# Cross-attention and ternary FFN on one core: squared queries in bf16 halves, a new order of every engine's two turns, weight chunks in two buffers

## The chip, the core and the metric

The kernel runs on one core of a Trainium2 chip. The metric is the device time of one execution in microseconds (us), lower is better. A core has TensorE (PE; its weight loads are listed as PEld), VectorE (DVE), ScalarE (ACT), GpSimd (POOL) and SyncE (SP), which issues every DMA here. Each engine works through its own list in order, and they meet at semaphores.

## The reference

```python
x = x + tanh(g_xattn[0]) * xattn(layernorm(x), ctx_1024, Wq, Wk, Wv, Wo, gq, gk)
x = x + tanh(g_ffn[0]) * ffn(layernorm(x), w_gate, w_up, w_down)

# xattn: 32 batch rows, 100 queries, 361 keys, 16 heads of 128
q = rmsnorm(hidden @ Wq, gq); k = rmsnorm(ctx @ Wk, gk); v = ctx @ Wv
out = softmax(q k^T / sqrt(D)) v @ Wo
# ffn: weights ternary: round(w / mean|w|) clipped to -1..1, times mean|w|
#      activations rounded to 8 bits per row; silu(gate) * up, then down
```

x is 32x100x512, ctx_1024 is 32x361x256, Wq is 512x2048, Wk and Wv are 256x2048, Wo is 2048x512, the three FFN matrices have 2048x512 elements each.

## The kernel before, in words

`attention_block` handles two batch rows (a pair) at a time, 16 pairs `i` in all; `ffn_block` follows. A factor of a product is held as a bf16 high half and a bf16 low half, and `product` makes three matmuls of them. A pair has 8 units: head group (4 heads) `u // 2` of batch row `u % 2`. While the values of unit `u` are mixed, unit `u+1` is scored and the keys of unit `u+2` are made, so that in turn `u` all three stages run. Two turns, odd `u` and `v = u + 1`, stand in one hand-written list per engine, `two_turns(i, u)`; a pair has four such double turns, `u` = 1, 3, 5, 7.

Keys of a unit are three tiles `t` (128, 128, 105 rows). PE: `keys`; ACT: `keys_square`; DVE: `sum_keys`; POOL: `key_scale` (two instructions); DVE: `scale_keys`; ACT: `keys_hi`; POOL: `keys_lo`; SP: `turn_keys`, a DMA transpose into `kT`; then PE may run `scores`. Query projections of a head group are made once in a double turn (`queries(i, u, 0)` and `1`), and `query_squares` sums the squares over the 128 partitions by a matmul: the f32 squares `qsq` are its weights, a column of ones is what moves. `query_squares_out` (DVE) and `query_scale` (POOL) make `qrs` of it, which `row_bias` of a later unit needs.

Queries, mixed values (`m`), head outputs (`o`), turned x (`x`) and squared-query sums (`qss`) take turns in two PSUM banks, `shared_ps`, in the order that `shared_uses` lists. `shared_bank` makes PE wait until the use two before has been read out (`shared_free`). In the double turn `u` = 3 the next pair's x is turned (`turn_x`), read out by `turn_x_hi` on ACT and `turn_x_lo` on DVE.

SP's list is `turn(i, u)`, one call for every unit: load a chunk, turn the context (in turns 5 and 6, `turn_ctx(i+1, b, ..)`, which `keys` of units 8 and 9 wait for through `ctxT_in`), turn keys, turn probabilities (`turn_probs`), and last `store_chunk`.

The FFN weights are made ternary beside attention, in 48 chunks of 128x512, one in a turn. In pairs 1 to 6 each chunk is loaded and its absolute values are summed (`weight_chunk` on ACT). In pairs 8 to 13 each is loaded again, scaled on ACT, clipped and rounded on POOL (`round_chunk`, w_rounded), and stored by SP (`store_chunk`), which first waits:

```python
sp.wait_ge(w_rounded, m + 1)
```

The lines that the rows name: L23 to L25 are the three matmuls of `product`; L527 the matmul of `query_squares`; L667 a copy to a high half on ACT; L716 `queries_square`; L877 a low half on DVE; L893 `scale_keys`; L917 `row_sum`; L923 `probs_lo`; L949 `layernorm`; L966 `query_squares_out`; L1181 `keys_lo`; L1221 and L1226 the clip and the rounding of `round_chunk`; L292 `turn_ctx`; L309 `turn_keys`; L372 `load_chunk`; L379 `store_chunk`.

## Time and profile before

| what | value |
| --- | --- |
| three runs | 2347.47 us median, 2344.13 to 2347.76 |
| the profiled execution | 2351.92 us, its span 2350.1 us, mean granted TensorE clock 0.977 |
| start and pair 0 | 0 to 210.9 us of the span |
| pairs 1 and 2 (chunks summed) | 210.92 to 455.61 us, 122.3 us a pair |
| pairs 3 to 7 (chunks summed until pair 6) | 455.61 to 1075.73 us, 124.0 us a pair |
| pairs 8 to 13 (chunks rounded) | 1075.73 to 1827.44 us, 125.3 us a pair |
| pairs 14 and 15 | 1827.44 to 1951.18 and 1951.18 to 2057.74 us |
| `ffn_block` | the last 292.4 us |

The borders of the pairs are the starts of the copies of the projected output (`project_out`), one couple of them at the end of each pair. The first row compares executions; everything else is of the one profiled execution. Matmuls overlap in the records, so that the cost of one is read from start to start, not from its duration. A few keys matmuls are missing in the records (136 to 137 of 144 stand in a pair); the time that they took is there as a hole without a releaser.

### The profile page before, as it was taken

The page shows a single profiled execution, that of the slowest core. Times are in us where ns is not written, and L with a number is a line of the kernel's source. Part 1 is how long each engine was busy: PE and PEld are TensorE (multiplying, and loading weights), DVE is VectorE, ACT ScalarE, POOL GpSimd, SP SyncE. Part 2 cuts the span into 40 slices and gives each one's busy share as a digit, 9 for nine tenths or more (in the row PEclk, how much of TensorE's full clock was granted, in tenths as well). Part 3 has the DMA queues.
Part 4 walks back from the last instruction along what each step waited for, and adds up shares of the span by engine and source line. Part 5 has one row for each costly group of instructions (what it writes and reads, how often), then busy time and mean ns, then how long its engine had stood idle before and what let it go on. Part 6 is the DMA issues. An engine that isn't in the chain of part 4 may idle for free. (4 is left out here: it accounts for less than half of the span.)

```text
span 2350.1 us, 45689 instructions
## 1 busy us (share of the span) xinstructions
PE 2215.9 (94%) x16187; PEld 1573.9 (67%) x16338; DVE 1837.9 (78%) x4171; ACT 1612.3 (69%) x3398; POOL 1273.9 (54%) x1623
## 2 busy tenths in 40 slices
PE   5889999999999999999999999999999999769999
PEld 3567777777776777777777777776767777534444
DVE  5788877787777787877777778777777777569997
ACT  4677777777776777666767777676767667546665
POOL 4555656565656555656666676767666655200000
PEclk9899999999999999999999999999999999989999
DMA  5776776666677776656676767676777665635665
GB/s 144 169 149 136 124 146 127 139 133 129 131 130 144 123 144 126 132 105 139 132 145 136 151 129 149 135 138 134 143 145 132 133 109 111 171 95 139 141 140 126
DMA packets 921748, 317.53 MB, mean 135 GB/s; under 512 B 864912, under 2 KB 882608, under 8 KB 921264
## 3 DMA queue, kind: packets, MB, share of 16 engines
q1 hardware_dynamic: 921520, 314.61, 66.6%
q8 instruction: 129, 2.11, 0.4%
q14 instruction: 99, 0.81, 0.1%
HBM read 82.09 MB, written 19.40 MB: 43 GB/s over the span
## 5 line engine op out<-in xcount | busy, mean ns | idle before, releaser
L1181 POOL TENSOR_TENSOR ksplit<-khat,ksplit 128x512 bf16<-128x512 f32 (+1 forms) x384 | 455.5, 1188 | 74.0 <-ACT ksplit L667 73.1
L893 DVE TENSOR_TENSOR khat<-keys_ps,krs 128x512 f32<-128x512 f32 (+1 forms) x384 | 263.4, 686 | 287.4 <-POOL krs L1175 287.2
L1175 POOL TENSOR_TENSOR krs<-kvar,minus_half 128x4 f32<-128x4 f32 (+1 forms) x384 | 387.1, 1008 | 32.0
L689 ACT ACTIVATE prob<-score_ps,nbias,qrs 100x361 f32<-100x361 f32 x512 | 328.6, 647 | 71.8 <-DVE nbias L911 70.4
L1172 POOL TENSOR_SCALAR kvar<-kss 128x4 f32<-128x4 f32 (+1 forms) x384 | 89.1, 232 | 531.9 <-DVE kss L883 530.0
L672 ACT ACTIVATE ksq<-keys_ps 128x512 f32<-128x512 f32 (+1 forms) x384 | 227.8, 596 | 188.5 <-PE keys_ps L25 188.4
L698 ACT ACTIVATE psplit<-prob,rden 100x361 bf16<-100x361 f32 x512 | 304.3, 595 | 64.9 <-DVE rden L917 64.2
L923 DVE SCALAR_TENSOR_TENSOR psplit<-prob,rden,psplit 100x361 bf16<-100x361 f32 x512 | 317.5, 629 | 4.2 <-ACT psplit L698 0.6
L901 DVE TENSOR_REDUCE nmax<-score_ps 100x1 f32<-100x361 f32 x512 | 268.3, 524 | 54.5 <-PE score_ps L25 54.3
L667 ACT ACTIVATE ksplit<-khat 128x512 bf16<-128x512 f32 (+1 forms) x384 | 240.5, 626 | 98.0 <-DVE khat L893 97.3
L24 PE MATMUL keys_ps<-wk_split,ctxT 128*128 128x512 bf16 (+1 forms) x768 | 293.8, 383 | 6.8
L25 PE MATMUL keys_ps<-wk_split,ctxT 128*128 128x512 bf16 x767 | 293.2, 382 | 0.0
L23 PE MATMUL keys_ps<-wk_split,ctxT 128*128 128x512 bf16 (+1 forms) x642 | 247.8, 386 | 33.3 <-DVE khat L893 18.3
L883 DVE TENSOR_REDUCE kss<-ksq 128x4 f32<-128x512 f32 (+1 forms) x384 | 259.6, 676 | 15.4 <-ACT ksq L672 15.2
L23 PE MATMUL shared_ps<-pT,nat 128*128 128x400 bf16 (+1 forms) x768 | 257.4, 335 | 10.7 <-DVE qT_lo L956 5.4
L23 PE MATMUL shared_ps<-xT_hi,wq_split 128*128 128x200 bf16 x1024 | 257.5, 251 | 9.6 <-DVE wq_split L877 5.7
L24 PE MATMUL shared_ps<-xT_lo,wq_split 128*128 128x200 bf16 x1024 | 257.6, 252 | 0.0
L25 PE MATMUL shared_ps<-xT_hi,wq_split 128*128 128x200 bf16 x1024 | 257.5, 251 | 0.0
L25 PE MATMUL shared_ps<-pT,nat 128*128 128x400 bf16 (+1 forms) x768 | 256.4, 334 | 0.0
L24 PE MATMUL shared_ps<-pT,nat 128*128 128x400 bf16 (+1 forms) x768 | 256.2, 334 | 0.0
L23 PE MATMUL y_ps<-oT_hi,wo_hi 128*128 128x200 bf16 x1024 | 255.0, 249 | 0.5 <-DVE oT_lo L877 0.5
L24 PE MATMUL y_ps<-oT_lo,wo_hi 128*128 128x200 bf16 x1024 | 255.0, 249 | 0.0
(132 smaller groups left out, 5323.1 us busy)
## 6 DMA issues: line engine op xcount, KB each, us to landing
stage<-in_ffn SPq DMA_DIRECT2D x96, 256.0 KB, 3.2
ctx_raw<-in_ctx SPq DMA_DIRECT2D x31, 256.0 KB, 3.5
xin<-in_x SPq DMA_DIRECT2D x32, 200.0 KB
res_rows<-in_x SPq DMA_DIRECT2D x32, 200.0 KB
x_rows<-res_rows SPq DMA_DIRECT2D x32, 200.0 KB
xin<-x_rows SPq DMA_DIRECT2D x25, 256.0 KB, 2.7
xres<-x_rows SPq DMA_DIRECT2D x25, 256.0 KB, 3.0
out<-xres SPq DMA_DIRECT2D x25, 256.0 KB, 2.0
```

The source lines that it names most:

```text
L23: pe.matmul(out, w_hi, m_hi, start=first, stop=False)
L24: pe.matmul(out, w_hi, m_lo, start=False, stop=False)
L25: return pe.matmul(out, w_lo, m_hi, start=False, stop=last)
L667: return act.activation(out, in_, ACT.Copy)
L689: act.activation(prob[:, h, :], score_ps[h % 2][0:SQ, 0:SK], ACT.Exp, bias=nbias[:, b, h:h + 1], scale=qrs[:, v // 2 % 2, r:r + 1], accum_ ...
L698: act.activation(psplit[0:SQ, h // TWO, 0, h % TWO, 0:SK], prob[:, h, :], ACT.Copy, scale=rden[:, b, h:h + 1]).then_inc(p_hi_done, 1)
L883: dve.tensor_reduce(kss[0:KV[t], k, :], ksq[0:KV[t], k, :].rearrange("p (h d) -> p h d", h=G), AX_X, ALU.add).then_inc(kss_done, 1)
L893: dve.tensor_tensor(khat[0:KV[t], k, :].rearrange("p (h d) -> p h d", h=G), keys_ps[k][0:KV[t], :].rearrange("p (h d) -> p h d", h=G), rs, ...
L901: dve.tensor_reduce(nmax[:, b, h:h + 1], score_ps[h % 2][0:SQ, 0:SK], AX_X, ALU.max, negate=True).then_inc(nmax_done, 1)
L923: dve.scalar_tensor_tensor(out=psplit[0:SQ, h // TWO, 1, h % TWO, 0:SK], in0=prob[:, h, :], scalar=rden[:, b, h:h + 1], in1=psplit[0:SQ, h ...
L1175: pool.tensor_tensor(krs[0:KV[t], k, :], kvar[0:KV[t], k, :], minus_half[0:KV[t], 0:G], ALU.pow).then_inc(krs_done, 1)
L1181: pool.tensor_tensor(ksplit[0:KV[t], t, 1, :], khat[0:KV[t], (u + t) % 2, :], ksplit[0:KV[t], t, 0, :], ALU.subtract).then_inc(k_lo_done, 1)
```

## The change

The squares of the queries are written twice by ACT: f32 into `qsq` (now only two heads, reused) and bf16 into `qsq_hi`; POOL subtracts them into the bf16 `qsq_lo`. `query_squares` multiplies high and low halves of 128 columns each. `qss` moves behind the head outputs. The lists of PE, ACT, DVE and POOL are put in a new order. Weight chunks use two buffers (stage slots 0 and 3) and are loaded a turn ahead; weight staging has 6 slots in place of 7. The context of batch row 0 is loaded for the pair after the next one at the end of turn 6, that of row 1 in turn 2.

```diff
             if more_queries(u, last):
-                order += [("q", u, 0)]
-            if more_queries(u, last):
-                order += [("q", u, 1)]
+                order += [("q", u, 0), ("q", u, 1)]
             order += [("m", u, 0), ("m", u, 1)]
             if u == UNITS - 5 and not last:
                 order += [("x", 0)]
-            if more_queries(u, last):
-                order += [("qss", u)]
             order += [("o", v, 0), ("o", v, 1)]
             if u == UNITS - 5 and not last:
                 order += [("x", 1)]
+            if more_queries(u, last):
+                order += [("qss", u)]
...
-    OWN_STAGES = 5
+    OWN_STAGES = 4
...
# SP: load_chunk, turn
             def load_chunk(i, u):
+                i, u = (i, u + 1) if u < UNITS else (i + 1, 1)
                 n, m = sum_chunk_of(i, u), tern_chunk_of(i, u)
-                if n is not None and n > 0:
-                    sp.wait_ge(w_summed, n)
-                if m is not None:
-                    sp.wait_ge(w_summed, MATRICES * CHUNKS)
-                    if m > 0:
-                        sp.wait_ge(w_rounded, m)
                 if n is not None or m is not None:
+                    c = n if m is None else MATRICES * CHUNKS + m
+                    if m is not None:
+                        sp.wait_ge(w_summed, min(c - 1, MATRICES * CHUNKS))
+                        if m > 1:
+                            sp.wait_ge(w_rounded, m - 1)
+                    elif n > 1:
+                        sp.wait_ge(w_summed, n - 1)
                     rows, cols = chunk_at(n if m is None else m)
-                    sp.dma_start(w_raw[:, :], w_ffn[rows, cols]).then_inc(w_raw_in, 16)
+                    sp.dma_start(w_raw[c % 2], w_ffn[rows, cols]).then_inc(w_raw_in[c % 2], 16)
...
                 if not last and u == 1:
-                    sp.wait_ge(nat_ready, (i * 2 + 2) * KVT)
-                    load_ctx(i + 1, 0, ctx_raw)
...
+                if not last and u == 2:
+                    sp.wait_ge(nat_ready, (i * 2 + 3) * KVT)
+                    load_ctx(i + 1, 1, ctx_raw)
+                if i < PAIRS - 2 and u == UNITS - 2:
+                    sp.wait_ge(nat_ready, (i * 2 + 4) * KVT)
+                    load_ctx(i + 2, 0, ctx_raw)
                 store_chunk(i, u)
...
# PE: query_squares
-                eng.wait_ge(q_sq_done, i * (NG * QD) + ((u + 3) // 2 + 1) * QD)
+                eng.wait_ge(q_sqlo_done, i * (NG * QD) + ((u + 3) // 2 + 1) * QD)
                 for b in range(2):
                     for h in range(G):
-                        last = pe.matmul(ps[0:SQ, b * G + h:b * G + h + 1], qsq[:, h, b * SQ:(b + 1) * SQ],
-                                         ones[:, 0:1], start=True, stop=True)
+                        out, hi, lo = ps[:, b * G + h:b * G + h + 1], h * QT + b * SQ, (G + h) * QT + b * SQ
+                        pe.matmul(out, qsq_split[:, hi:hi + P], ones[:, 0:1], start=True, stop=False)
+                        last = pe.matmul(out, qsq_split[:, lo:lo + P], ones[:, 0:1], start=False, stop=True)
...
# ACT and POOL: the new passes
+            def queries_square_hi(i, u, k):
+                n, p = use(i, ("q", u, k))
+                ps, heads = shared_ps[p][:, 0:TWO * QT].rearrange("p (h q) -> p h q", h=TWO), slice(k * TWO, (k + 1) * TWO)
+                eng.wait_ge(shared_done, n + 1)
+                act.activation(qsq_hi[:, heads, :], ps, ACT.Square).then_inc(q_sqhi_done, 1)
...
+                eng.wait_ge(q_sq_done, n)
+                eng.wait_ge(q_sqhi_done, n)
+                pool.tensor_tensor(qsq_lo[:, heads, :], qsq[:, :, :], qsq_hi[:, heads, :],
+                                   ALU.subtract).then_inc(q_sqlo_done, 1)
```

The order of a double turn after the change, the lists written without their conditions (`u` and `v = u + 1`; keys are those of `u+2` and `v+2`, scores, maxima and probabilities those of `u+1` and `v+1`):

```
PE    keys u:0, u:1; queries 0; scores 0; queries 1; keys u:2; scores 1, 2; keys v:0; mixed u 0, 1;
      scores 3; keys v:1; [turn_x 0]; heads_out 0, 1; [turn_x 1]; keys v:2; query_squares;
      scores v 0, 1; project 0 to 3; scores v 2, 3; mixed v 0, 1
DVE   sum u:0, u:1; row_max 0, row_bias 0; scale u:0, u:1; queries_lo 0; sum u:2; row_max 1, row_sum 0,
      row_bias 1; queries_lo 1; scale u:2; row_max 2; [layernorm 0]; row_sum 1; sum v:0; row_bias 2;
      mixed_lo 0; row_max 3; mixed_lo 1; row_bias 3, probs_lo 0, row_sum 2; scale v:0; [layernorm 1];
      probs_lo 1, row_sum 3; [turn_x_lo 0]; heads_out_lo 0; probs_lo 2, 3; heads_out_lo 1; [turn_x_lo 1]; ...
POOL  key_scale u:0, u:1, keys_lo u:0; query_squares_lo 0; key_scale u:2, keys_lo u:1, u:2;
      key_scale v:0; [split_ctx 0]; query_squares_lo 1; [split_ctx 1, 2]; keys_lo v:0,
      key_scale v:1, v:2; keys_lo v:1, v:2; round_chunk u; query_scale; round_chunk v
```

In brackets stands what one double turn of a pair alone has. Before, PE ran `query_squares` ahead of `heads_out`, `keys v:0` between the two `mixed`, and `scores 0, 1` together; POOL had `round_chunk u` behind `key_scale v:0` and `query_scale`, ahead of all three `keys_lo v`.

## Rows read from the trace of the kernel before

**Rows 1.** The page's first part: busy time, share of the span, instructions.
```profile
PE 2215.9 (94%) x16187; PEld 1573.9 (67%) x16338; DVE 1837.9 (78%) x4171; ACT 1612.3 (69%) x3398; POOL 1273.9 (54%) x1623
```

**Rows 2.** Windows, three groups of pairs: length, busy PE, PEld, DVE, ACT, POOL; clock; DMA.
```profile
210.92:455.61 244.69, 238.50 (x1875) 178.48 (x1889) 194.95 (x449) 178.07 (x405) 148.40 (x186) 1.00 0.70 135
455.61:1075.73 620.12, 606.86 (x4693) 455.58 (x4732) 488.52 (x1124) 442.20 (x996) 370.92 (x461) 0.98 0.68 130
1075.73:1827.44 751.71, 725.69 (x5630) 543.85 (x5677) 584.81 (x1345) 532.95 (x1164) 508.31 (x646) 0.99 0.71 140
```

**Rows 3.** Waits of PE in pairs 8 to 13: us in total, times, longest.
```profile
PE shared_ps L23 <- DVE qvar L966: 7.6, 6, 2.3
PE keys_ps L23 <- DVE khat L893: 7.3, 11, 1.1
...
PE shared_ps L23 <- DVE xT_lo L877: 4.1, 6, 0.7
```

**Rows 4.** Groups of weight loads by shape: busy us, mean ns, idle before.
```profile
L25 PEld LDWEIGHTS y_ps<-oT_hi,wo_lo 128*128 128x128 bf16 x1024 | 100.2, 98 | 0.0
...
L24 PEld LDWEIGHTS score_ps<-kT,qT_hi 128*100 128x100 bf16 x512 | 64.3, 126 | 12.5 <-issue 0.2
```

**Rows 5.** Timeline of PE: start, length; first and last of 24 output projections.
```profile
1011.43 0.25 PE L23 MATMUL y_ps<-oT_hi,wo_hi 128*128 128x200 bf16 x1
...
1013.41 0.25 PE L25 MATMUL y_ps<-oT_hi,wo_lo 128*128 128x200 bf16 x1
```

**Rows 6.** Timeline of PE: a burst of squared-query matmuls and what follows it.
```profile
1593.86 1.49 PE L527 MATMUL shared_ps<-ones,qsq 128*100 128x1 f32 x16
1595.21 0.25 PE L23 MATMUL shared_ps<-uT,wv_hi 128*128 128x200 bf16 x1
```

**Rows 7.** Windows: behind the burst of pair 7's turn 3, and in pair 15.
```profile
1003.00:1009.80 6.80, 6.27 (x35) 5.29 (x35) 4.21 (x10) 2.63 (x5) 5.28 (x6) 0.50 0.47 90
...
2044.05:2050.88 6.83, 5.52 (x17) 2.49 (x18) 0.57 (x1) 0.50 (x1) 0.00 (x0) 0.50 0.98 317
```

**Rows 8.** Timeline of PE: the longest idle stretch of pair 15 ends.
```profile
2045.36 0.49 PE L23 MATMUL shared_ps<-pT,nat 128*128 128x400 bf16 x1 [5.29 <-DMA pT<-psplit]
```

**Rows 9.** Timeline of POOL: a chunk's rounding at the end of turn 6, pair 12.
```profile
1671.22 1.16 POOL L1181 TENSOR_TENSOR ksplit<-khat,ksplit 105x512 bf16<-105x512 f32 x1 [0.34 <-ACT ksplit L667]
...
1673.53 0.70 POOL L1226 TENSOR_SCALAR w_out<-stage 128x512 bf16<-128x512 f32 x1 [0.16 <-POOL stage L1221]
```

**Rows 10.** Timeline of PE: second keys matmul of turn 7, and its first scores.
```profile
1674.58 0.38 PE L24 MATMUL keys_ps<-wk_split,ctxT 128*128 128x512 bf16 x1
...
1679.01 0.32 PE L23 MATMUL score_ps<-kT,qT_hi 128*100 128x361 bf16 x1
```

**Rows 11.** Timeline of SP's queue: the end of turn 5 and the start of turn 6.
```profile
1666.03 0.41 SPq L379 DMA_DIRECT2D w_tern<-w_out  x1
...
1667.03 3.81 SPq L292 DMA_TRANSPOSE ctxT<-nat  x3
1670.93 3.98 SPq L309 DMA_TRANSPOSE kT<-ksplit  x3
```

**Rows 12.** DMA issues: count, median us from issue to landing.
```profile
ctxT<-nat SPq DMA_TRANSPOSE x96, 3.0
```

**Rows 13.** Groups by line, ACT, POOL and DVE: busy us, mean ns, idle before.
```profile
L716 ACT ACTIVATE qsq<-shared_ps 128x400 f32<-128x400 f32 x128 | 64.4, 503 | 108.6 <-PE shared_ps L25 108.6
...
L1181 POOL TENSOR_TENSOR ksplit<-khat,ksplit 128x512 bf16<-128x512 f32 (+1 forms) x384 | 455.5, 1188 | 74.0 <-ACT ksplit L667 73.1
...
L923 DVE SCALAR_TENSOR_TENSOR psplit<-prob,rden,psplit 100x361 bf16<-100x361 f32 x512 | 317.5, 629 | 4.2 <-ACT psplit L698 0.6
...
L893 DVE TENSOR_TENSOR khat<-keys_ps,krs 128x512 f32<-128x512 f32 (+1 forms) x384 | 263.4, 686 | 287.4 <-POOL krs L1175 287.2
...
L949 DVE TENSOR_SCALAR xin<-xin,ln_mv,ln_rstd 100x512 f32<-100x512 f32 x32 | 18.8, 590 | 0.0
...
L877 DVE TENSOR_TENSOR xT_lo<-shared_ps,xT_hi 128x400 bf16<-128x400 f32 x32 | 18.2, 569 | 1.6 <-ACT xT_hi L667 1.2
```

More of the change, by code:

```diff
@@ L116, in use, with query_use @@
         return i * USES + k, k % 2
+    def query_use(i, u):
+        n = i * UNITS + u // 2 * 2 - 3
+        return use(n // UNITS, ("q", n % UNITS, QD - 1))[0]
     def unit(i, u):
@@ L406, in turn @@
                         load_x(i + 1, b, xin, x_in)
-                if not last and u == 3:
-                    sp.wait_ge(nat_ready, (i * 2 + 3) * KVT)
-                    load_ctx(i + 1, 1, ctx_raw)
                 if not last and u in (UNITS - 3, UNITS - 2):
@@ L601, in two_turns @@
                 if su:
-                    scores(i, u + 1, 0), scores(i, u + 1, 1)
+                    scores(i, u + 1, 0)
+                if qu:
+                    queries(i, u, 1)
                 if ku:
                     keys(i, u + 2, 2)
-                if qu:
-                    queries(i, u, 1)
                 if su:
-                    scores(i, u + 1, 2)
-                mixed(i, u, 0, par)
+                    scores(i, u + 1, 1), scores(i, u + 1, 2)
+                if kv:
+                    keys(i, v + 2, 0)
+                mixed(i, u, 0, par), mixed(i, u, 1, par)
                 if su:
                     scores(i, u + 1, 3)
-                if kv:
-                    keys(i, v + 2, 0)
-                mixed(i, u, 1, par)
                 if kv:
@@ L1046, in two_turns @@
                     layernorm(i, 0)
-                if qu:
-                    queries_lo(i, u, 1)
                 if su:
-                    row_max(i, u + 1, 3), row_bias(i, u + 1, 2), row_sum(i, u + 1, 1), probs_lo(i, u + 1, 0)
-                    row_bias(i, u + 1, 3)
-                mixed_lo(i, u, 0)
+                    row_sum(i, u + 1, 1)
                 if kv:
@@ L1055, in two_turns @@
                 if su:
-                    probs_lo(i, u + 1, 1), row_sum(i, u + 1, 2)
+                    row_bias(i, u + 1, 2)
+                mixed_lo(i, u, 0)
+                if su:
+                    row_max(i, u + 1, 3)
                 mixed_lo(i, u, 1)
+                if su:
+                    row_bias(i, u + 1, 3), probs_lo(i, u + 1, 0), row_sum(i, u + 1, 2)
                 if kv:
                     scale_keys(i, v + 2, 0)
+                if new_x:
+                    layernorm(i, 1)
                 weights_lo(pieces_of(i, u, 1))
+                if su:
+                    probs_lo(i, u + 1, 1), row_sum(i, u + 1, 3)
                 if new_x:
-                    layernorm(i, 1), turn_x_lo(i, 0)
-                if qu:
-                    query_squares_out(i, u)
+                    turn_x_lo(i, 0)
+                weights_lo(pieces_of(i, u, 2)), heads_out_lo(i, v, 0)
                 if su:
-                    row_sum(i, u + 1, 3), probs_lo(i, u + 1, 2)
-                if kv:
-                    sum_keys(i, v + 2, 1)
-                if su:
-                    probs_lo(i, u + 1, 3)
-                weights_lo(pieces_of(i, u, 2))
-                heads_out_lo(i, v, 0), heads_out_lo(i, v, 1)
+                    probs_lo(i, u + 1, 2), probs_lo(i, u + 1, 3)
+                heads_out_lo(i, v, 1)
+                if new_x:
+                    turn_x_lo(i, 1)
                 if i == TERN_PAIR - 1 and u == 1:
                     weight_scales()
-                if new_x:
-                    turn_x_lo(i, 1)
                 if u == 1 and not last:
@@ L1079, in two_turns @@
                 if sv:
-                    row_max(i, v + 1, 0), row_bias(i, v + 1, 0), row_max(i, v + 1, 1), row_bias(i, v + 1, 1)
+                    row_max(i, v + 1, 0)
+                if kv:
+                    sum_keys(i, v + 2, 1)
+                if sv:
+                    row_bias(i, v + 1, 0)
                 if kv:
@@ L1093, in two_turns @@
                 if sv:
-                    probs_lo(i, v + 1, 0), probs_lo(i, v + 1, 1), row_sum(i, v + 1, 2), row_sum(i, v + 1, 3)
+                    probs_lo(i, v + 1, 0), row_sum(i, v + 1, 2), row_sum(i, v + 1, 3), probs_lo(i, v + 1, 1)
                 weights_lo(pieces_of(i, v, 1))
@@ L1204, in split_ctx @@
                     eng.wait_ge(ctx_in[b], (j + 1) * 32)
-                    if not (isinstance(j, int) and j == 0):
-                        eng.wait_ge(shared_done, use(j - 1, ("m", 1, CC - 1))[0] + 1)
+                    if j > 1:
+                        eng.wait_ge(shared_done, use(j - 2, ("m", UNITS - 1, CC - 1))[0] + 1)
                 pool.tensor_copy(nat[0:KV[t], par, b, t, 0, :], raw[0:KV[t], t, :]).then_inc(nat_hi_done, 1)
```

201 lines of the change are left out of this document (114 added, 87 removed).

## The prediction

> **What bounds the kernel now.** I read the page first: PE is busy for 94% of the span, no other engine over 78% [rows 1]. Durations of matmuls overlap, so I went on to the windows by pair: PE stands idle for some 3% of a pair (6.2 of 244.7 us in pairs 1 and 2, 26.0 of 751.7 in pairs 8 to 13), while DVE is busy for 78 to 80% and ACT for 71 to 73% [rows 2]. Attention is bound by PE's list, and a change is worth what it takes out of PE's starts and PE's idle time. A pair takes 122.3, 124.0 and 125.3 us in the three groups. The middle group differs from the first by the granted clock (0.98 against 1.00), the last by waits. The waits of PE in the last group are 23.4 us in six pairs, 3.9 a pair, with the wait of the squared-query matmul on `mixed_lo` (0.7 us in each pair); the largest kinds are in [rows 3]. The same view gives 2.3 a pair for the others, of the same kinds.
>
> **The cheaper squares.** A burst of 16 f32 matmuls with one moving column takes 1.35 us from its start to the next group's start [rows 6], 84 ns each; there are 64 bursts, so 86 us. The new burst has 16 bf16 matmuls too, each behind a load of 128 columns. No row shows such loads back to back. From above: among 200-column matmuls a load of 128 hides wholly, and these follow each other by 1.98 / 23 = 86 ns [rows 5]; from below only nothing bounds it. A burst costs 0.91 us. Gain 64 x 0.44 = 28 us; ends -2 (a loss) and 86.
>
> The Trainium skill (TensorE: Matmul & The Clock Gate, Weight-path perf modes) says that the fast weight load is on when the number of weights is 128 and the type is not FP32, measured at about twice the speed. The trace agrees with the direction (98 against 126 ns). By the page's other figure, a plain load of one column in 1/1.2 ns, half of 107 ns for 128 columns is an estimate of 53 ns, and a gain of 32 us.
>
> **The added passes.** ACT gets one more Square of 503 ns for each query use [rows 13], 8 a pair, 4.0 us on some 88 of 125 busy. POOL gets 8 subtractions of 400 columns, 1188 x 400/512 = 0.93 us each [rows 13], 7.4 us a pair on 508.3 / 6 = 84.7 [rows 2]. Neither bounds a pair. DVE gets nothing. What is exposed is order, so I walked a double turn with the durations of the rows. From keys u:0 at 0 us, without stalls, PE runs scores 0 at 4.7, mixed 0 at 10.7, scores 3 at 13.7, the head outputs at 15.5 and 16.5, keys v:2 at 17.6, the squares at 18.9 and ends at 28.6. `mixed_lo` 1 ends at 15.5 on DVE, khat u:0, u:1, u:2 and v:0 at 6.8, 7.5, 12.2 and 17.1: each just ahead of its reader. An ordinary double turn has no stall over some 0.2 us; uncovered, each of these would cost its lateness once a double turn.
>
> **The turn with the new x (u = 3).** Here a wait is added. `heads_out` 1 stands two uses behind `turn_x` 0 in the shared banks, so it waits for `turn_x_lo` 0. On DVE this stands behind `mixed_lo` 1 with row_bias 3, probs_lo 0, row_sum 2, scale v:0, layernorm 1, probs_lo 1 and row_sum 3 between: 0.2 + 0.63 + 0.15 + 0.69 + 0.59 + 0.63 + 0.15 = 3.0 us, then 0.57 of its own [rows 13]. `mixed_lo` 1 ends at 16.0 in this double turn (a layernorm lies ahead of it), so the bank is free at 19.6, and PE wants it at 17.0: 2.6 us, where before the same place cost 0.73 + 0.69 (4.1 us in six pairs behind xT_lo [rows 3]). Small stalls of the other double turns I put at 0.5. So 3.1 a pair against 2.3: +0.8 in eight pairs without rounding (1 to 7 and 14) is +6 us. Bounds: 0.5 and 5 a pair.
>
> **The clock.** Behind the burst of `u` = 3 the granted clock is 0.50, its lower level of 1.2 GHz, for 6.8 us, in which the 24 head-output matmuls run [rows 7]: 24 x 86 ns = 2.1 us lost. Ahead of it PE had four transposes, a wait, the burst with one moving column, and another wait. It happens in pairs 3 to 14, so 12 x 2 = 24 us less a few that overlap idle time: 22. The change moves the burst away from the transposes, but sets an idle 2.6 us near them. I take half of it: gain 11, ends 0 and 22.
>
> **The queue behind the rounding.** This is the step that speaks against the change. `store_chunk(i, u)` makes SP wait for `w_rounded` at the end of turn u, and everything of turn v is queued behind: in turn 6 three `turn_ctx`, in each turn v three `turn_keys`, and `turn_probs`. Before, the rounding of chunk u stood ahead of `keys_lo v`. Now POOL reaches it only behind `keys_lo` v:2. Before, that very slot held the rounding of chunk v: keys_lo ends at 1672.4, the rounding at 1674.23 [rows 9], while the next double turn starts at 1674.58 - 0.21 = 1674.37 [rows 10]. So w_rounded now comes about when the next double turn starts; I move it 0.6 us earlier, for keys v:2 ends 9.9 us before the end in place of some 9.2. From the store to the third context transpose's issue SP takes 1.0 + 2/3 x 3.81 = 3.5 us [rows 11], and landing takes 3.0 [rows 12], 6.5 in all, while keys u:0 of turn 7 (unit 9) need all three. Stall: 6.5 - 0.1 - 0.6 = 5.8; since the trace also shows shorter landings in this place I take 5.2. In the other three double turns the queue has the store, a load and three key transposes, 6.6 us, and the first scores stand 4.64 us behind the start [rows 10]: 6.6 - 0.6 - 4.6 = 1.4 at most, less in the first double turn, where `keys_lo` ends earlier; I take 0.8, so 2.4. An idle 5.29 us in pair 15 [rows 8] was followed by 0.50 for 6.83 us, 5.5 of them busy [rows 7]: 2.7 lost; I take 2.0. Sum 9.6 us a pair; with the 3.1 above 12.7, against 3.9 before: +8.8, six pairs, +53 us. Ends of the 9.6: 0 where the transposes land in time after all, and 6.3 + 3.4 + 3 x 2.0 = 15.7.
>
> The Trainium skill (TensorE: Matmul & The Clock Gate, Why this matters for your kernels) wants no idle gap of TensorE over about 3 us, lest the clock falls back to half. The trace agrees (5.29 us idle, then 0.50), and by this rule the wait of turn 7 costs more than its idle time.
>
> **The rest.** Double chunk buffers: ACT never waited for a chunk, so nothing. The context two turns ahead takes a wait of POOL away, which reached PE as a part of the 7.6 us behind qvar [rows 3]; that is inside the 3.9 that I replace. Six staging slots in place of seven and the extra passes in the start: +2 us, ends 0 and 6. `ffn_block` is untouched.
>
> Sum: -28 + 6 - 11 + 53 + 2 = +22 us on the profiled 2351.9, so 2374; the median of the runs is 0.19% lower, so 2369.5, rounded to 2369.
>
> **Rivals** (times on the scale of the median). (1) The other side: the transposes behind the rounding land in time, because POOL gets to it earlier than in my walk. Then the rounding pairs get 3.1 - 3.9 = -0.8 each and the sum is -36: 2311. For it: DVE and ACT have slack of a fifth; against: the slot of [rows 9]. It decides where the queue costs under 6.0 us a pair rather than 9.6. (2) The queue costs its upper end, 15.7: +36 us more, 2405. (3) The walk is wrong in `u` = 3: no long wait for xT_lo, and the clock stays up: -2 x 15 - 11 = -41, 2328. For it, two waits of 0.7 there became one; against, seven instructions on DVE. (4) Full-width loads are no faster: 28 us more, 2397; the 98 ns speak against it. (5) The change doesn't do what it might for the clock: 0.50 behind the turned x in every pair, 11 more, 2380. (6) The in-order lists stall by themselves, 2 us a pair: 30 more, 2399.
>
> **How the numbers follow.** Chances: forecast (2350 to 2390) 0.36, (1) 0.20, (2) 0.12, (3) 0.12, (4) 0.06, (5) 0.08, (6) 0.06. The range 2300 to 2405 reaches to (1) and (2). A measurement of this kernel tells about 0.2%, 4.7 us, from no change. Faster: (1) 0.20, of (3) 0.10, of the forecast 0.02: 0.32. Same: 0.10, of the forecast's lower edge and of (3). Slower: the rest, 0.58.
>
> **What would show it.** In the profile after: 16 squared-query matmuls in some 1.0 us; in pairs 8 to 13 a wait of `keys_ps` L23 on the DMA ctxT<-nat of about 5 us, one a pair, with clock 0.50 behind it, and waits of `score_ps` on the DMA kT<-ksplit; none of these in pairs 1 to 7; one wait of `shared_ps` on xT_lo of 2 to 3 us a pair; pairs without rounding at some 119 to 121 us, those with it at about 133. The forecast is wrong first of all if SP's queue isn't what PE waits for in pairs 8 to 13.

## The result, and the profile after

The kernel after takes 2487.53 us (median of 4 runs, 2480.23 to 2491.64) against 2345.8 of the kernel before (4 runs, 2342.74 to 2347.76): a ratio of 1.0602, 95% interval 1.0573 to 1.0631. It is slower, as forecast, but by 142 us in place of 22, and it lies far above the range of 2300 to 2405.

The first part of the page after, for [rows 1]:

```profile
PE 2210.0 (89%) x16338; PEld 1517.1 (61%) x16338; DVE 1970.1 (79%) x4171; ACT 1666.7 (67%) x3526; POOL 1366.9 (55%) x1752
```

PE is busy for about as long as before, in a span of 2485.0 us in place of 2350.1: what came in is idle time. The windows of the same groups of pairs, for [rows 2] (length, busy PE, PEld, DVE, ACT and POOL, granted clock, DMA share, GB/s):

```profile
209.80:460.71 250.91, 234.82 (x1893) 171.00 (x1892) 214.20 (x450) 184.90 (x419) 158.51 (x202) 0.99 0.73 132
460.71:1083.60 622.89, 587.72 (x4733) 428.83 (x4732) 528.28 (x1125) 458.23 (x1037) 395.18 (x501) 0.99 0.71 129
1083.60:1958.99 875.39, 748.70 (x5679) 532.61 (x5677) 642.12 (x1345) 556.71 (x1213) 546.60 (x693) 0.94 0.62 119
```

Start and pair 0 lost nothing (209.8 against 210.9 us), pairs 1 to 7 lost 9.0 us (873.8 against 864.8), the six pairs that round chunks lost 123.7 (875.4 against 751.7, or 145.9 a pair in place of 125.3), pairs 14 and 15 another 3.3. That is 134.9 with the start, the whole difference of the spans. Where the six pairs lost it stands in the waits of PE in them (us in total, times, longest), for [rows 3]:

```profile
PE keys_ps L23 <- DMA ctxT<-nat: 50.3, 12, 5.6
PE score_ps L23 <- DMA kT<-ksplit: 41.4, 19, 3.4
PE shared_ps L23 <- DVE xT_lo L899: 14.0, 6, 2.3
PE shared_ps L23 <- DVE qT_lo L980: 13.1, 18, 0.7
PE shared_ps L23 <- DVE uT L899: 7.9, 18, 0.6
```

Together 126.7 us where there were 23.4: 103.3 more. The squares gave back 24 x 0.95 = 22.8 us (below). The other 43.2 us go with the clock: at a mean of 0.94 in place of 0.99, 0.06 x 875.4 - 0.01 x 751.7 = 45.0 us more of such loss is an estimate. A run below, `e9_combined_ctx`, has the same matmuls in these pairs at a mean of 1.00, and there PE is busy for 701.9 us in place of 748.7: 46.8 less. In pairs 1 to 7 the same view reads:

```profile
PE shared_ps L23 <- DVE xT_lo L899: 16.3, 7, 2.3
PE shared_ps L23 <- DVE uT L899: 11.7, 25, 0.6
PE shared_ps L23 <- DVE qT_lo L980: 11.4, 15, 1.1
PE keys_ps L23 <- DMA ctxT<-nat: 8.7, 9, 1.7
PE score_ps L23 <- DMA kT<-ksplit: 3.1, 4, 1.2
```

51.2 us, some 7.3 a pair where before had 2.3: +35, against 28 x 0.95 = 26.6 saved by the squares. So two things have to be explained: the DMA waits of the rounding pairs, and small waits on DVE in every pair.

The queue, at the end of turn 2 of pair 11. POOL first (start, length), then SP's queue, then PE:

```profile
1550.94 2.27 POOL L1217 TENSOR_TENSOR ksplit<-khat,ksplit 128x512 bf16<-128x512 f32 x2
1553.30 0.91 POOL L1266 TENSOR_SCALAR stage<-stage 128x512 f32<-128x512 f32 x1
1554.36 0.62 POOL L1271 TENSOR_SCALAR stage<-stage 128x512 bf16<-128x512 f32 x1 [0.16 <-POOL stage L1266]
```

```profile
1555.01 0.35 SPq L395 DMA_DIRECT2D w_tern<-stage  x1
1555.47 0.37 SPq L388 DMA_DIRECT2D stage<-in_ffn  x1
1555.93 3.96 SPq L319 DMA_TRANSPOSE kT<-ksplit  x3
```

```profile
1553.85 0.38 PE L23 MATMUL keys_ps<-wk_split,ctxT 128*128 128x512 bf16 x1
...
1562.04 0.54 PE L23 MATMUL score_ps<-kT,qT_hi 128*100 128x361 bf16 x1 [3.37 <-DMA kT<-ksplit]
```

The last `keys_lo` ends at 1553.21, the rounding at 1554.98, and the three key transposes, two of whose tiles had been ready for 8 and 3 us, are issued only behind the store. PE reaches the first scores at 1558.67 and waits for 3.37 us. Then the window around it has the lower level of the clock:

```profile
1561.17:1568.00 6.83, 5.96 (x30) 4.86 (x31) 2.47 (x5) 1.86 (x4) 3.17 (x4) 0.50 1.05 215
```

The new burst of squares, for [rows 6], and what follows it:

```profile
857.71 0.17 PE L547 MATMUL shared_ps<-ones,qsq_split 128*128 128x1 bf16 x1
857.74 0.16 PE L548 MATMUL shared_ps<-ones,qsq_split 128*128 128x1 bf16 x1
...
858.09 0.16 PE L548 MATMUL shared_ps<-ones,qsq_split 128*128 128x1 bf16 x1
858.11 0.34 PE L23 MATMUL score_ps<-kT,qT_hi 128*100 128x361 bf16 x1
```

16 matmuls, each behind a load of 128 columns, in 0.40 us, 25 ns each, where the f32 burst took 1.35 (its eight f32 matmuls stand in the trace as 16 records, 84 ns each). That is 0.95 us less, 64 x 0.95 = 61 us.

### The profile page after: what moved, and what is told of

It reads as the page before. It is cut to its first block and busy times, and to the rows that moved or that the text cites. A ratio compares the mean times of both kernels' runs of the same rounds, so it can differ in the third digit from the quotient of the medians.

```text
span 2485.0 us, 46479 instructions
## 1 busy us (share of the span) xinstructions
PE 2210.0 (89%) x16338; PEld 1517.1 (61%) x16338; DVE 1970.1 (79%) x4171; ACT 1666.7 (67%) x3526; POOL 1366.9 (55%) x1752
## 5 line engine op out<-in xcount | busy, mean ns | idle before, releaser
L1217 POOL TENSOR_TENSOR ksplit<-khat,ksplit 128x512 bf16<-128x512 f32 (+1 forms) x384 | 446.3, 1164 | 387.8 <-ACT ksplit L683 383.7
L23 PE MATMUL keys_ps<-wk_split,ctxT 128*128 128x512 bf16 (+1 forms) x768 | 304.7, 397 | 81.9 <-DMA ctxT<-nat 76.8
L945 DVE SCALAR_TENSOR_TENSOR psplit<-prob,rden,psplit 100x361 bf16<-100x361 f32 x512 | 323.9, 643 | 16.1 <-ACT psplit L714 16.1
L714 ACT ACTIVATE psplit<-prob,rden 100x361 bf16<-100x361 f32 x512 | 297.5, 594 | 32.1 <-DVE rden L939 25.3
L24 PE MATMUL keys_ps<-wk_split,ctxT 128*128 128x512 bf16 (+1 forms) x768 | 303.0, 395 | 0.0
L25 PE MATMUL keys_ps<-wk_split,ctxT 128*128 128x512 bf16 (+1 forms) x768 | 301.2, 392 | 0.0
L933 DVE TENSOR_TENSOR nbias<-nmax,qrs 100x1 f32<-100x1 f32 x512 | 276.6, 540 | 13.9 <-DVE nmax L923 0.5
L23 PE MATMUL shared_ps<-xT_hi,wq_split 128*128 128x200 bf16 x1024 | 263.3, 257 | 10.0 <-DVE wq_split L899 6.2
L24 PE MATMUL shared_ps<-xT_lo,wq_split 128*128 128x200 bf16 x1024 | 263.1, 257 | 0.0
L25 PE MATMUL shared_ps<-xT_hi,wq_split 128*128 128x200 bf16 x1024 | 262.9, 257 | 0.0
L1208 POOL TENSOR_SCALAR kvar<-kss 128x4 f32<-128x4 f32 (+1 forms) x384 | 74.6, 194 | 335.6 <-DVE kss L905 335.1
```

Of the source, the lines that this page charges most:

```text
L23: pe.matmul(out, w_hi, m_hi, start=first, stop=False)
L24: pe.matmul(out, w_hi, m_lo, start=False, stop=False)
L25: return pe.matmul(out, w_lo, m_hi, start=False, stop=last)
L714: act.activation(psplit[0:SQ, h // TWO, 0, h % TWO, 0:SK], prob[:, h, :], ACT.Copy, scale=rden[:, b, h:h + 1]).then_inc(p_hi_done, 1)
L933: dve.tensor_tensor(nbias[:, b, h:h + 1], nmax[:, b, h:h + 1], qrs[:, v // 2 % 2, r:r + 1], ALU.mult).then_inc(nbias_done, 1)
L945: dve.scalar_tensor_tensor(out=psplit[0:SQ, h // TWO, 1, h % TWO, 0:SK], in0=prob[:, h, :], scalar=rden[:, b, h:h + 1], in1=psplit[0:SQ, h ...
```

## The experiments

Each ratio is of the kernel to the kernel before, with its 95% interval; the kernel before was timed again for each group of runs (medians of 2350.8 to 2352.2 us). "After" is 2487.5 us, 1.0602.

| run | edit | us | ratio |
| --- | --- | --- | --- |
| `e1_store_behind_keys` | after; store u and the load of turn v behind the transposes of turn v | 2349.2 | 0.9987 (0.9971 to 1.0004) |
| `e2_rounding_early` | after; chunk u scaled and rounded where it was before | 2361.0 | 1.0065 (1.0041 to 1.0089) |
| `e3_swap_dve` | after; queries_lo 1 ahead of row_bias 1 | 2455.2 | 1.0442 (1.0414 to 1.0471) |
| `e4_xlo_early` | after; turn_x_lo 0 ahead of layernorm 1 | 2460.9 | 1.0468 (1.0441 to 1.0496) |
| `e14_short_keys_lo` | after; one keys_lo of six cut to a quarter | 2423.9 | 1.0308 (1.0272 to 1.0344) |
| `e6_hundred_columns` | after; loads of 100 columns | 2493.2 | 1.0601 (1.0569 to 1.0633) |
| `e5_old_order` | bf16 squares in the lists of before | 2447.5 | 1.0410 (1.0386 to 1.0434) |
| `e10_old_lo_early` | e5; query_squares_lo 1 earlier on POOL | 2386.6 | 1.0148 (1.0117 to 1.0180) |
| `e11_old_squares_late` | e10; squares behind the head outputs | 2367.5 | 1.0063 (1.0043 to 1.0083) |
| `e8_combined_two_out` | e1 + e3 + e4, two buffers for rounded chunks | 2310.8 | 0.9832 (0.9811 to 0.9853) |
| `e9_combined_ctx` | e8; context transposes of row 0 in turn 4 | 2296.0 | 0.9770 (0.9751 to 0.9788) |
| `e12_f32_added` | e9; the old f32 burst ahead of each new one | 2387.5 | 1.0158 (1.0132 to 1.0184) |

**The queue, from SP's side and from POOL's.**

```diff
# e1: SP, turn
-                load_chunk(i, u)
+                if u % 2:
+                    load_chunk(i, u)
...
                     turn_keys(i, u + 2, 0), turn_keys(i, u + 2, 1), turn_keys(i, u + 2, 2)
+                if u % 2 == 0:
+                    store_chunk(i, u - 1)
+                    load_chunk(i, u)
...
-                store_chunk(i, u)
+                if u % 2 == 0:
+                    store_chunk(i, u)
```

> The kernel after, with one thing moved in SP's list: the store of chunk u and the load of the turn v = u + 1 stand behind the context and key transposes of turn v, ahead of its probability transposes, in place of ahead of all of turn v. Queue theory (the transposes of turn v were queued behind the wait for w_rounded): in pairs 8 to 13 the waits of PE for the DMAs ctxT and kT, 18 us in pair 11, mostly go, and the low clock behind them with them; those pairs fall from 146 us to 125 to 130, so 6 x 16 to 21 us less, 2360 to 2390 us in all. Rival (the rounding passes and copies overload ACT or POOL, or their place delays keys_lo, whatever SP does): the rounding pairs stay above 140 us, the total above 2450. Both: pairs 1 to 7 stay at 124.5 us, and the wait for xT_lo of 2.3 us a pair stays.

```diff
# e2: POOL, two_turns; the scaling on ACT likewise, to behind the last weights_hi of turn u
+                round_chunk(i, u)
                 if kv:
                     keys_lo(i, v + 2, 0), key_scale(i, v + 2, 1), key_scale(i, v + 2, 2)
...
-                round_chunk(i, u)
                 if qu:
                     query_scale(i, u)
                 round_chunk(i, v)
```

> The kernel after, with SP's list unchanged and the rounding of chunk u back at its place of before on POOL (ahead of the three keys_lo of turn v) and the scaling of chunk u back at its place of before on ACT (behind the last weight copy of turn u). Queue theory: w_rounded comes in time for SP's wait, so the stalls on ctxT and kT in pairs 8 to 13 go as in the kernel before, those pairs fall to 125 to 130 us, the total to 2360 to 2390; a little may be lost where the rounding pushes keys_lo. Rival (it is the order of SP's own list, or the two new passes, and not the time of the rounding): the stalls on ctxT and kT stay, total above 2450.

Moving the store and the load behind it in SP's list takes 138 us away, bringing the rounding back on POOL and ACT takes 127; the first total is 11 us under the range expected, the second in it (2360 to 2390), and the rival is out of both. In the profiles 125.6 and 116.3 us of this lie in the six rounding pairs. Another 9.3 and 10.9 lie in pairs 1 to 7, where nothing is rounded, though both edits move something there too (the loads in e1, the sums on ACT in e2); no run tells what made those. The six rounding pairs of e1 (in length 125.0 us a pair), and then PE's waits in them:

```profile
1072.02:1821.77 749.75, 702.41 (x5632) 514.90 (x5678) 633.37 (x1345) 552.81 (x1213) 546.96 (x693) 0.99 0.74 140
```

```profile
PE keys_ps L24 <- DMA ctxT<-nat: 14.4, 6, 3.1
PE shared_ps L23 <- DVE xT_lo L904: 13.9, 6, 2.3
PE shared_ps L23 <- DVE qT_lo L985: 8.7, 12, 0.7
PE shared_ps L23 <- DVE uT L904: 8.0, 18, 0.6
```

The waits for kT are gone, those for ctxT are six in place of twelve (the ones in turn 7 went), the waits for xT_lo and uT are as they were, and the clock is back at 0.99. So it is neither the work on POOL and ACT nor its place by itself: it is that transposes stand in line behind a wait for a late rounding.

**The small waits on DVE.** In turn 3 of pair 10, DVE, POOL and PE of the kernel after:

```profile
1421.78 0.15 DVE L939 RECIPROCAL rden<-den 100x1 f32<-100x1 f32 x1
1421.89 2.04 DVE L933 TENSOR_TENSOR nbias<-nmax,qrs 100x1 f32<-100x1 f32 x1
1423.85 0.62 DVE L980 SCALAR_TENSOR_TENSOR qT_lo<-shared_ps,gqk,qT_hi 128x400 bf16<-128x400 f32 x1
```

```profile
1421.79 1.01 POOL L1211 TENSOR_TENSOR krs<-kvar,minus_half 105x4 f32<-105x4 f32 x1
1422.76 1.16 POOL L1217 TENSOR_TENSOR ksplit<-khat,ksplit 128x512 bf16<-128x512 f32 x1
```

```profile
1424.53 0.34 PE L23 MATMUL shared_ps<-pT,nat 128*128 128x400 bf16 x1 [0.73 <-DVE qT_lo L980]
```

A `row_bias` of one column, 0.15 us by itself, starts inside one POOL instruction and ends with the next one; `queries_lo` 1 stands behind it, and mixed 1 on PE waits for that. 52 `row_bias` of the kernel after last over 1.9 us, none of the kernel before does.

```diff
# e3: DVE, two_turns
-                    row_max(i, u + 1, 1), row_sum(i, u + 1, 0), row_bias(i, u + 1, 1)
+                    row_max(i, u + 1, 1), row_sum(i, u + 1, 0)
...
                 if qu:
                     queries_lo(i, u, 1)
+                if su:
+                    row_bias(i, u + 1, 1)
```

> The kernel after, with two neighbours of DVE's list swapped: queries_lo 1 ahead of row_bias 1. In the kernel after this row_bias of one column lasts 2.04 us, while two POOL instructions run beside it, and ends with them; queries_lo 1 behind it makes mixed 1 on PE wait 0.73 us in nearly every double turn. Theory that DVE's row_bias is held until POOL's instruction is over: queries_lo 1 runs 2 us earlier, the 0.73 goes in all of some 55 double turns (about 40 us, if nothing else takes its place), row_bias still ends with POOL's instruction. Rival (the hold passes to queries_lo, or row_max and the exponentials behind it become late instead): the wait stays or moves, the time changes by less than 10 us.

```diff
# e14: POOL, two_turns; keys_lo has the number of columns as its last argument (the low half of the rest is left out)
-                    key_scale(i, u + 2, 2), keys_lo(i, u + 2, 1), keys_lo(i, u + 2, 2)
+                    key_scale(i, u + 2, 2), keys_lo(i, u + 2, 1, P), keys_lo(i, u + 2, 2)
```

> The kernel after, with the second keys_lo of each double turn (tile 1 of unit u + 2) cut to 128 of its 512 columns, so that the low half of three heads of that tile is left out. In the kernel after, row_bias 1 lasts 2.04 us, from inside POOL's krs to the end of this keys_lo. Theory that POOL's running instruction holds DVE's row_bias: the row_bias now ends where the short keys_lo ends, some 0.8 us earlier, and the wait of mixed 1 for qT_lo (0.73 us) goes: some 30 us less in all, about 5 a pair in pairs 1 to 7. Rival (row_bias waits on its own inputs or on ACT): its length stays 2.04 us and the wait stays.

The swap gave 32 us of the 40 expected. The shorter POOL instruction gave 64, twice the 30 expected: the waits for qT_lo went, and those for uT nearly so (in pairs 1 to 13 from 19.6 to 3.2 us), as if the whole list on DVE behind the held one had moved up. All `row_bias` of a kernel in one row (ns, shortest, median, longest); in order the kernels before, after and `e14_short_keys_lo`:

```profile
L911 DVE TENSOR_TENSOR nbias<-nmax,qrs x512: 143/160/1118, 47.8 to 2037.6; 100x1 f32<-100x1 f32 x171
```

```profile
L933 DVE TENSOR_TENSOR nbias<-nmax,qrs x512: 143/163/2076, 47.7 to 2172.2; 100x1 f32<-100x1 f32 x171
```

```profile
L933 DVE TENSOR_TENSOR nbias<-nmax,qrs x512: 145/160/1172, 47.2 to 2102.5; 100x1 f32<-100x1 f32 x171
```

The same `row_bias` of turn 3, pair 10, in `e14_short_keys_lo`, DVE and then POOL:

```profile
1416.92 0.38 DVE L933 TENSOR_TENSOR nbias<-nmax,qrs 100x1 f32<-100x1 f32 x1
1417.22 0.62 DVE L980 SCALAR_TENSOR_TENSOR qT_lo<-shared_ps,gqk,qT_hi 128x400 bf16<-128x400 f32 x1
```

```profile
1416.81 1.01 POOL L1211 TENSOR_TENSOR krs<-kvar,minus_half 105x4 f32<-105x4 f32 x1
1417.79 0.43 POOL L1217 TENSOR_TENSOR ksplit<-khat,ksplit 128x128 bf16<-128x128 f32 x1
```

The length on DVE follows what POOL runs, with DVE's own inputs unchanged: the rival of e14 is out. The theory has its end wrong, though. The `row_bias` doesn't last until the short `keys_lo` is over: it ends at 1417.30, 0.92 us ahead of that and still inside krs, and so is 1.66 us shorter and not 0.8, which goes with the doubled gain. Why the length of the next POOL instruction decides this isn't shown.

**The turn with the new x, and the clock.**

```diff
# e4: DVE, two_turns
                 if new_x:
-                    layernorm(i, 1)
+                    turn_x_lo(i, 0), layernorm(i, 1)
...
-                if new_x:
-                    turn_x_lo(i, 0)
```

> The kernel after, with turn_x_lo 0 on DVE moved ahead of layernorm 1 and probs_lo 1 in the double turn u = 3. The order theory (heads_out 1 waits for that read-out because seven instructions stand ahead of it): the wait of 2.3 us falls to some 0.6 us, 15 pairs x 1.7 = 26 us less; and if that idle stretch is what lowered the clock in about half of the pairs (1.7 us lost each), up to 12 us more, so 2450 to 2461 us. Rival (xT_hi on ACT is itself late, or layernorm 1 and turn_x 1 become the wait): under 8 us less. If the clock's fall comes from the transposes and not from the wait, the low stretch stays.

27 us less, at the edge of what was expected (2450 to 2461): the wait for xT_lo fell from 2.3 to 0.7 us in each pair, and PE got new ones of 0.4 and 0.3 behind it. The clock tells more than the total. In four of pairs 1 to 7 the kernel after has a stretch at 0.50 right behind that wait; the first of them, and then all seven pairs of e4:

```profile
386.99:390.40 3.41, 3.20 (x18) 2.83 (x19) 2.57 (x5) 1.14 (x3) 1.15 (x3) 0.50 0.55 103
```

```profile
208.98:1075.50 866.52, 816.13 (x6568) 594.53 (x6623) 740.85 (x1573) 642.37 (x1455) 554.34 (x702) 1.00 0.72 131
```

In those pairs e4 has no such stretch behind that wait, and one behind another, in pair 1. The four transposes are still there, so here the fall goes with the idle 2.3 us beside them. How often it comes isn't settled by that wait alone: with the same 2.3 us it comes in four of pairs 1 to 7 in the kernel after, in three in e1 and in all seven in e3. Nor is the wait the only way to it. `e12_f32_added` (below) has waits of 0.7 us and less in this place and the f32 burst back on PE, and in eight of pairs 1 to 13 a stretch at 0.50 right behind that burst; `e9_combined_ctx`, the same without the f32 burst, has none there. The one in pair 5 of e12:

```profile
777.64:781.05 3.41, 3.41 (x20) 2.71 (x19) 2.94 (x8) 1.79 (x5) 1.64 (x4) 0.50 0.47 90
```

**The squares by themselves.** Two edits on the burst, and the new squares in the lists of before.

```diff
# e6: PE, query_squares
-                        out, hi, lo = ps[:, b * G + h:b * G + h + 1], h * QT + b * SQ, (G + h) * QT + b * SQ
-                        pe.matmul(out, qsq_split[:, hi:hi + P], ones[:, 0:1], start=True, stop=False)
-                        last = pe.matmul(out, qsq_split[:, lo:lo + P], ones[:, 0:1], start=False, stop=True)
+                        out, hi, lo = ps[0:SQ, b * G + h:b * G + h + 1], h * QT + b * SQ, (G + h) * QT + b * SQ
+                        pe.matmul(out, qsq_split[:, hi:hi + SQ], ones[:, 0:1], start=True, stop=False)
+                        last = pe.matmul(out, qsq_split[:, lo:lo + SQ], ones[:, 0:1], start=False, stop=True)
```

> The kernel after, with squared-query loads of 100 columns in place of 128 (the output then has 100 partitions). If the full width is what makes the bursts cheap (25 ns from one matmul to the next), the burst of 16 goes back towards the 84 ns of the f32 one, from 0.4 to 1.0 to 1.4 us, 64 bursts, 38 to 64 us more: 2520 to 2550. Rival (bf16 alone makes it cheap, whatever the width): the burst stays at 0.4 to 0.6 us and the total within 10 us of the kernel after.

```profile
862.13 0.17 PE L547 MATMUL shared_ps<-ones,qsq_split 128*100 128x1 bf16 x1
...
862.86 0.34 PE L23 MATMUL score_ps<-kT,qT_hi 128*100 128x361 bf16 x1
```

0.73 us a burst, 46 ns a matmul: of the 0.95 us, bf16 alone does 0.62 and the full width 0.33. Neither theory had that. 64 x 0.33 = 21 us more were to be expected from it, and the total moved by 6, inside its interval. In pairs 1 to 7 the time is there: 883.6 us in place of 873.8, 9.8 more where 28 x 0.33 = 9.2. In pairs 8 to 13 it is not: they take 867.9 in place of 875.4, with PE's waits the same (125.6 against 126.7) and the clock at 0.95 in place of 0.94, which by an estimate (0.01 x 870) gives some 9 us back.

```diff
# e12: PE, query_squares, ahead of the bf16 burst
+                for b in range(2):
+                    for h in range(G):
+                        pe.matmul(ps[0:SQ, b * G + h:b * G + h + 1], qsq[:, h % TWO, b * SQ:(b + 1) * SQ],
+                                  minus_half[:, 0:1], start=True, stop=True)
```

> The best kernel so far (2296 us) with the f32 burst of the kernel before put ahead of each bf16 burst: eight f32 matmuls with one moving column, which read the f32 squares of two heads and whose result the bf16 burst overwrites. It prices a burst where it stands. Theory that the burst is on PE's path: 64 x 1.35 = 86 us more, 2382. Rival (its place hides it, so that the trace's start-to-start times say nothing of the gain): under 30 us more.

91.5 us more, 1.43 a burst. Some 18 us of it are the clock's (means 0.979 and 0.986: 0.021 x 2384.1 - 0.014 x 2293.5, an estimate), and PE's waits in pairs 1 to 13 got 10.9 us shorter (39.4 against 50.3). That leaves 90.6 - 18 + 10.9 = 84 us in the profiles, 1.3 a burst: on PE's path the time from start to start is what a burst costs, and the f32 burst really was worth some 86 us.

```diff
# e5: the four two_turns, shared_uses and context loads of before, and in the lists of ACT and POOL
-                    queries_square(i, u, 1), queries_hi(i, u, 1)
+                    queries_square_hi(i, u, 1), queries_square(i, u, 1), queries_hi(i, u, 1)
...
-                    query_scale(i, u)
+                    query_squares_lo(i, u, 1), query_scale(i, u)
```

> The bf16 squares with their two added passes, the two chunk buffers and the memory layout of the kernel after, but the lists of PE, ACT, DVE and POOL, the order of the shared banks and the context loads of the kernel before; the high squares stand ahead of the f32 squares on ACT, query_squares_lo 0 behind the first keys_lo on POOL and query_squares_lo 1 ahead of query_scale. Theory that the squares by themselves gain what their bursts say (a burst of 0.4 us in place of 1.35, 64 bursts, 60 us) and that the new order is what takes it back: 2285 to 2300 us. Rival (the added passes cost as much by themselves, or PE waits for query_squares_lo 1 ahead of the head outputs, since the squares stand early in this order): 2320 to 2350 us, with a wait of shared_ps on qsq_split in each double turn.

The rival won, and by more than it asked for: 2447. POOL, and the burst on PE:

```profile
558.91 0.47 POOL L1200 TENSOR_SCALAR kvar<-kss 128x4 f32<-128x4 f32 x1 [1.18 <-DVE kss L909]
559.46 1.01 POOL L1203 TENSOR_TENSOR krs<-kvar,minus_half 128x4 f32<-128x4 f32 x1
560.43 0.94 POOL L1218 TENSOR_TENSOR qsq_split<-qsq,qsq_split 128x400 bf16<-128x400 f32 x1
```

```profile
561.52 0.16 PE L546 MATMUL shared_ps<-ones,qsq_split 128*128 128x1 bf16 x1 [2.09 <-POOL qsq_split L1218]
```

POOL idles for 1.18 us for `key_scale` v:0 while the subtraction stands behind it. Two more runs moved first the subtraction, then also the burst:

```diff
# e10: POOL, two_turns
                     key_scale(i, u + 2, 2), keys_lo(i, u + 2, 1), keys_lo(i, u + 2, 2)
+                if qu:
+                    query_squares_lo(i, u, 1)
...
-                    query_squares_lo(i, u, 1), query_scale(i, u)
+                    query_scale(i, u)
# e11: PE, two_turns; shared_uses, query_squares_out and query_scale as in the kernel after
-                if qu:
-                    query_squares(i, u)
                 heads_out(i, v, 0), heads_out(i, v, 1)
...
                     keys(i, v + 2, 2)
+                if qu:
+                    query_squares(i, u)
```

> The kernel with the old order and the bf16 squares, with query_squares_lo 1 moved on POOL from behind key_scale v:0 to ahead of it, directly behind keys_lo u:2. With the old order PE waited 2.1 to 4.3 us for query_squares_lo 1 in each of 63 bursts, 154 us in all, and POOL stood idle 1.2 us ahead of key_scale v:0 meanwhile. Theory that only POOL's slot was late: the wait goes wholly or nearly, and the low clock behind it (3.4 us in many pairs), so 2280 to 2310 us. Rival (the chain queries 1, Square twice, subtraction is too long for squares that stand ahead of the head outputs, wherever POOL has it): a wait of over 1 us stays in each double turn, 2340 to 2400.

> The same, and the squared-query matmuls moved behind the head outputs and keys v:2, as in the kernel after, with their read-out on DVE and query_scale on POOL at the places of the kernel after. Theory that the late squares are the one part of the new order that the bf16 squares need: no wait for qsq_split, pairs at 119 to 121 us, total 2270 to 2295 us. Rival (something else in the old order waits for the squares' place, such as row_bias for qrs, or the old order needs the rest of the new one): over 2310.

Both missed: 2387 and 2367 us, the totals of their rivals. The wait for qsq_split is gone (which the rival of e10 had staying), but in its place PE waits for uT ahead of the head outputs (e11, its pairs 8 to 13):

```profile
PE shared_ps L23 <- DVE uT L903: 26.4, 24, 2.1
PE shared_ps L23 <- DVE xT_lo L903: 5.9, 6, 1.0
```

So in the old order more is lost than the cheap burst gives, and these waits are part of it. What makes the uT copies late there, the two added Squares on ACT or DVE behind POOL, no run told apart, nor what the chunk buffers and the start add.

**Together.**

```diff
# e8: e1, e3, e4, and (the waits of the store and of the rounding likewise)
-        w_raw, w_out = [stage[:, 0, :], stage[:, 3, :]], stage[:, 2, 0:CHUNK // 2].bitcast(BF16)
+        w_raw = [stage[:, 0, :], stage[:, 3, :]]
+        w_out = [stage[:, 2, 0:CHUNK // 2].bitcast(BF16), stage[:, 1, CHUNK // 2:CHUNK].bitcast(BF16)]
# e9: e8, and in SP's turn
-                if not last and u in (UNITS - 3, UNITS - 2):
+                if not last and u == UNITS - 2:
                     sp.wait_ge(keys_done, tile(i, u + 1, KVT - 1) + 1)
-                    turn_ctx(i + 1, u - (UNITS - 3), 1 - par)
+                    turn_ctx(i + 1, 1, 1 - par)
...
+                if not last and u == UNITS - 4:
+                    sp.wait_ge(keys_done, tile(i, u + 2, KVT - 1) + 1)
+                    turn_ctx(i + 1, 0, 1 - par)
```

> The kernel after with three of the single edits together: the store of chunk u behind the transposes of turn v, queries_lo 1 ahead of row_bias 1, and turn_x_lo 0 ahead of layernorm 1; and the rounded chunks go to two buffers in turn, so that the rounding of chunk v doesn't wait for the store of chunk u. If the three losses are independent: 138 + 32 + 27 us less than the kernel after, 2290 us; two buffers matter only if the store makes POOL late, which no trace shows so far, so 0 to 3 more. Rival (they overlap, each stall hiding behind the next one): 2310 to 2330.

> The same, with the context transposes of batch row 0 moved in SP's list from the start of turn 5 to the end of turn 4, behind its probability transposes. In the runs so far PE waits for them 0.4 to 3.1 us in every pair, in the double turn u = 5. Queue theory: this wait goes, 15 x 1.3 = 20 us less than the run without the move, and the low clock behind the longest ones too. Rival (the three transposes delay the key transposes of turn 5 instead, and scores wait): no gain.

The three gains add to 197 us and gave 177 together, with the second buffer, which was not priced alone: 2310.8 is at the edge of the rival's range, so they overlap. The moved context transposes gave 15 of 20 us. e9 is the fastest kernel here, 2.3% under the kernel before, with rounding pairs of 121.4 us:

```profile
1050.71:1778.91 728.20, 701.86 (x5679) 511.63 (x5677) 608.73 (x1345) 544.62 (x1213) 544.24 (x693) 1.00 0.77 145
```

## Why the prediction was right in its direction and wrong in its size

- **PE's list bounds the kernel.** Right: e12 put 64 bursts on it and each cost about its full time.
- **The cheaper squares, -28 us.** The mechanism holds, the size was off. The term "57 ns" measured 25, so the gain is 61 us. 57 came from a load rate that no row showed; between 0 and 86 ns nothing pointed to it. The other estimate of the prediction, 53 ns, is likewise twice what was measured.
- **The added passes: "An ordinary double turn has no stall over some 0.2 us".** This step failed. PE waited 0.73 us for qT_lo and 0.55 for uT in most double turns, 44.1 us in pairs 1 to 13 (13.1 + 7.9 + 11.4 + 11.7). My walk gave `row_bias` its usual 0.2 us; beside POOL it took up to 2.08 in the kernel after, and e3 and e14 showed that this was what PE waited for. These waits took back most of what the squares gave, so that pairs without rounding came at 124.8 us and not at 119 to 121. Rival (6), lists that stall by themselves, was true as well, at more than its 2 us a pair.
- **u = 3.** Right: 2.6 us predicted, 2.33 measured in each pair, at the place named.
- **The clock in u = 3, half of it back.** Too much: 11 us were taken and 3.4 came. Of the low stretches in this place the kernel before has one in each of pairs 3 to 13, 3.4 us long in nine of them and 6.8 in two (I had read 6.8 in all, and pair 14 too), 22.2 us lost at half the clock. The kernel after has 11 as well, in pairs 2, 3, 5, 7 and in each of 8 to 14, all of 3.4 us, 18.8 lost. That the total of 22 for before came out is luck. e4 showed the idle 2.3 us beside the transposes to bring the fall, and e12 the f32 burst with much shorter waits. The clock thus also fell behind idle times shorter than those that the rule named in the prediction asks to avoid.
- **The queue behind the rounding, +53 us.** The step was right in its place and its mechanism (e1, e2) and far too small: the six pairs lost 123.7 us, and taking the queue away gave 125.6 in them. By its own terms: the context wait of turn 7 measured 5.5 us (5.2 taken). The key waits were 2.5, 3.4 and 1.9 us in pair 11, not 0.8. A third wait of 1.5 to 4.1 us, for the context of batch row 0 in turn 5, stood in no term. The DMA waits thus came to 15.3 us a pair for 7.6. The clock's share, taken as 2.0 us a pair behind one long wait, was 7: nearly each double turn now has a wait of about 2 us or more, and the clock falls behind many of them. So the step came to some 22 us a pair where it had 9.6, with an upper end of 15.7. Of the key waits, my own bound was 1.4 us and I took 0.8 without a row for it. Store to last landing takes 6.98 us in the turn shown, not 6.6. Chunk u is rounded 0.1 to 0.5 us ahead of the next double turn in 14 of the 24 double turns and 1.1 to 1.4 ahead in the last one of each pair, where I had 0.7. In the other four, all at the end of turn 2 as in the rows above, it comes 1.0 to 1.1 us behind, and the wait is 3.2 to 3.4: there all three `split_ctx` and a `deviation` stand on POOL ahead of the last `keys_lo`, and I hadn't walked that turn for itself (in pairs 10 and 12 PE had just waited another 1.5 us, so that POOL had caught up).
- **The range.** Its upper end took the queue's end alone. The two things that went wrong, a longer queue and held DVE instructions, can happen together, and the clock adds to both.

The Trainium skill (SBUF — State Buffer, SBUF: two separate sides) has DVE and GpSimd share a pair of SBUF ports by an exclusive lock, held for a whole instruction, that a DVE instruction with two SBUF inputs needs as well. The traces agree in part. In the kernel after each of the 124 `nbias` that start inside a `keys_lo`, with over 0.2 us of it left, ends within 0.02 us of it, and there is no such hold on `rden` (0.15 us), which has one input. But of the 157 that start so inside krs 105 take their usual 0.16 us, and the other 52 are those of 2.04; in the kernel before none of 87 is held there. The rule doesn't have that difference, and the measurement decides. Had I weighed it in the walk, `row_bias` ahead of `queries_lo` 1 would still have stood out as a risk.

## What to carry to other kernels

Before moving a producer later in its engine's list, list everything that stands behind the instruction that waits for it in the DMA queue, and walk each kind of turn for itself: here one store in the wrong place cost some 6%, and moving it and a load behind the transposes brought the kernel back to the time of before. A cheaper instruction that needs more passes to feed it must be priced with their place in the lists: in the old order it lost, and the new order with it and with the mends of e8 and e9 is 2.3% under the kernel before (54 us, where the bursts by themselves are worth 61). In a walk, give small DVE instructions with two SBUF inputs the length of the POOL instruction that runs beside them, and keep them from standing ahead of a read-out that frees a PSUM bank.
